# Batch 1's keys and positions loaded a stage ahead, query splits behind the maxima, and layer 1's queries as two 64-column products

## The reference

```python
# layer 1: 16 heads of 64
query = einsum('btd,dnh->bnth', q, w_query) + b_query
weights = softmax(einsum('bnth,bnsh->bnts', query, key) / sqrt(64))
out = einsum('bnth,ndh->btd', weights @ value, w_projection) + b_projection
# layer 2: 16 heads of 8, scores + bias by key position, explicit mask, softmax with a sink of 1
e = exp(scores - max(scores)); attn = e / (1 + sum(e))
# layer 3: 16 heads of 8, triangular and padding mask, plain softmax
```

## Time and profile before

| | us |
|---|---|
| median of 3 runs (lowest, highest) | 1465.39 (1463.68, 1467.89) |
| the profiled execution's own time | 1463.88 |
| its span | 1462.1 |
| busy: PE / DVE / ACT / POOL | 1284.2 / 996.0 / 811.8 / 687.8 |

### The profile page before, as it was taken

The page is one execution under the profiler, slowest core; times in us unless marked ns, Lnnn a source line. Parts: engine busy times, 40 slices in busy tenths (PEclk is TensorE's granted clock), DMA queues, the critical chain, the costliest instruction groups (busy, mean ns, idle before and its releaser), DMA issues. The chain is left out here.

```text
span 1462.1 us, 32229 instructions
## 1 busy us (share of the span) xinstructions
PE 1284.2 (88%) x11864; PEld 764.0 (52%) x11872; DVE 996.0 (68%) x3093; ACT 811.8 (56%) x1191; POOL 687.8 (47%) x630
## 2 busy tenths in 40 slices
PE   6999968836999999999984499999799966999994
PEld 4444444632666666666663145555467752555542
DVE  4988846136667666766557588888365676888866
ACT  2777732333656565656544367777553312777773
POOL 4667613521667667766762445241150027545411
PEclk8999987975999999999996689999999995999997
DMA  4556553534544144323003855440130005534301
GB/s 156 189 221 228 205 200 107 168 101 146 222 152 167 38 159 159 116 86 146 2 1 61 178 125 137 119 122 15 50 59 1 1 8 110 101 78 85 62 7 30
DMA packets 91078, 157.73 MB, mean 108 GB/s; under 512 B 15529, under 2 KB 60740, under 8 KB 87343
## 3 DMA queue, kind: packets, MB, share of 16 engines
q1 hardware_dynamic: 86440, 126.39, 29.8%
q10 hardware_dynamic: 2688, 25.56, 4.5%
q0 software_dynamic: 1808, 3.83, 1.2%
HBM read 99.16 MB, written 50.62 MB: 102 GB/s over the span
## 5 line engine op out<-in xcount | busy, mean ns | idle before, releaser
L2106 DVE CUSTOM_DVE_ANT_0 a_junk<-a_psM,a_madd 128x512 bf16<-128x512 f32 x480 | 312.9, 686 | 64.5 <-issue 57.7
L2049 ACT ACTIVATE a_probs<-a_psE 128x1024 f32<-128x1024 f32 x256 | 262.0, 1024 | 102.2 <-PE a_psE L1907 98.4
L2493 DVE TENSOR_REDUCE a_mx<-a_psM 128x1 f32<-128x512 f32 x236 | 148.2, 669 | 124.4 <-PE a_psM L2317 124.4
L1872 PE MATMUL a_psM<-narrow_k_op,narrow_q_op 57*64 57x512 bf16 (+1 forms) x960 | 194.1, 410 | 13.9 <-DMA narrow_q_op<-a_y_parts 8.7
L2454 ACT ACTIVATE a_probs<-a_psE 128x1024 f32<-128x1024 f32 x128 | 130.8, 1024 | 85.9 <-PE a_psE L2339 82.6
L2287 POOL TENSOR_TENSOR a_half_sum<-a_probs 128x1024 f32<-128x1024 f32 x64 | 150.7, 2355 | 32.7 <-ACT a_probs L2454 32.7
L1919 PE MATMUL a_psO<-a_probs,narrow_values 128*32 128x256 f32 x2048 | 163.7, 393 | 1.2 <-ACT a_probs L2049 1.2
L1898 PE MATMUL a_psE<-narrow_q_op,narrow_k_op 60*64 60x256 bf16 (+1 forms) x2048 | 155.4, 281 | 10.1 <-DMA narrow_q_op<-a_max_parts 10.1
L1907 PE MATMUL a_psE<-a_maddT,res_identb 64*64 64x512 bf16 x512 | 149.2, 386 | 0.0
L1907 PE MATMUL a_psE<-a_maddT_cross,res_identb 64*64 64x512 bf16 x512 | 147.1, 386 | 0.0
L2335 PE MATMUL a_psE<-a_qT,a_kT 64*128 64x256 f32 x1024 | 134.0, 381 | 0.0
(11 more groups left out here) (395 smaller groups left out, 2658.7 us busy)
## 6 DMA issues: line engine op xcount, KB each, us to landing
wide_k<-a_k_stage SPq DMA_DIRECT2D x32, 512.0 KB, 2.6
a_k_part<-wide_k SPq DMA_DIRECT2D x64, 256.0 KB, 2.9
wide_v<-a_v_stage SPq DMA_DIRECT2D x24, 512.0 KB, 4.1
a_kT<-wide_k ACTq DMA_DIRECT2D x6, 2048.0 KB
a_values<-wide_v ACTq DMA_DIRECT2D x6, 2048.0 KB, 8.5
keys<-a_parts SPq DMA_DIRECT2D x96, 64.0 KB
narrow_k_op<-keys SPq DMA_DIRECT2D x30, 192.0 KB
narrow_q_op<-a_queries SPq DMA_DIRECT2D x28, 192.0 KB
```

Source lines behind the costliest of these rows:

```text
L1872: last = pe.matmul(max_bank(s, j, first)[c * n:(c + 1) * n, :], q_op[r][group, s // 2, s % 2 * P + c * n:s % 2 * P + (c + 1) * n], k_op[r] ...
L2049: act.activation(probs[:, head:head + 2, k:k + 2, :], psE[es % 2][:], ACT.Exp).then_inc(exped, 1)
L2106: dve.tensor_tensor_reduce(junk[j][:], max_bank(s, j, first), madd[r][:, t, :], 1.0, -3.0e38, ALU.add, ALU.max, mx[r][:, max_place(h, t):m ...
L2493: dve.tensor_reduce(mx[r][:, at:at + 1], max_bank(2 * p + t, j, first), AX.X, ALU.max).then_inc(max_read, 1)
```

## The change

Three edits. (1) In both narrow layers batch 1's keys (and in layer 2 its positions) are loaded in the stage before, counted by `first_keys`; SP's later list loses them, and batch 1's context and turned mask move behind `maxima(0, 0)`. (2) POOL's `split_queries(v+2)` moves from ahead of `split_max(v, 1)` to the end of the iteration, behind `own_masks(v+2)`. (3) Layer 1's query is two products of 64 columns in two column tiles.

```diff
 # NarrowConstants.sync (int8 block), at its end, before its waits
+        nb.load_keys(sp, self.keys, 1, 1, nb.first_keys)
+        nb.load_positions(sp, 1, 1, nb.first_keys)
 # MaskConstants.gpsimd (layer 2's experts)
-        nb.load_keys(pool, self.keys, 0, 0, nb.first_keys)
+        for u in range(2):
+            nb.load_keys(pool, self.keys, u, u, nb.first_keys)
 # narrow_attention, SP
                 load_mask(1)
-                load_keys(1)
-                load_context(1)
                 load_queries(1)
                 cross_masks(0)
-                load_maskT(1)
 ...
                     maxima(v, 0)
+                    if v == 0:
+                        load_maskT(1)
+                        load_context(1)
 # narrow_attention, POOL
-                    if v + 2 < NCHUNK:
-                        split_queries(v + 2)
                     if cfg.q_bias:
                         bias_batch(v)
                     split_max(v, 1)
                     if v >= 1:
                         normalise(v - 1)
                     if v + 2 < B:
                         own_masks(v + 2)
+                    if v + 2 < NCHUNK:
+                        split_queries(v + 2)
 # narrow_attention, PE
-                            pe.wait_ge(nb.first_keys, 16 * n_keys)
-                        pe.wait_ge(loaded[r], 16 * (n_loads * turn + n_first if r == 0 else n_loads * (turn + 1)))
+                            pe.wait_ge(nb.first_keys, 2 * 16 * n_keys)
+                        pe.wait_ge(loaded[r], 16 * (n_loads * turn + (n_first, 2, n_loads)[r]))
 # layer1_attention, PE
                 def query(v, p):
-                    pe.matmul(psQ, wq[:, p * P:(p + 1) * P], res.xnT[:, bass.ds(v * S, S)], start=True, stop=True).then_inc(q_made, 1)
+                    for j in range(2):
+                        at = p * P + j * WIDE_E
+                        last = pe.matmul(psQ[j * WIDE_E:(j + 1) * WIDE_E, :], wq[:, at:at + WIDE_E], res.xnT[:, bass.ds(v * S, S)],
+                                         start=True, stop=True, tile_position=(0, j * WIDE_E), skip_group_check=True)
+                    last.then_inc(q_made, 1)
```

## The result

| | before | after |
|---|---|---|
| median (lowest, highest), 4 runs each | 1464.54 (1462.42, 1467.89) | 1450.34 (1448.32, 1452.49) |
| span of the profiled execution | 1462.1 | 1448.7 |
| busy: PE / DVE / ACT / POOL | 1284.2 / 996.0 / 811.8 / 687.8 | 1277.3 / 994.8 / 812.1 / 691.7 |

The ratio is 0.9913, 95% interval 0.989 to 0.9936: 12.7 us faster by it, 14.2 by the medians, where 22.6 was forecast. The sign was right and the time inside the range, but it lies 8 us above the forecast and outside the likeliest case's own range, beyond the 1447 that the prediction gave as its own sign of being wrong. Rival B's time, about 1449, is the nearest.

The account below looks back on a forecast made before the run. PE was taken to bound layer 1's attention, and PE's waits on the DMA queue and POOL to cost the narrow layers. Gains of 28.4 less costs of 5.8 gave 22.6 us: 1441.3, stated as 1442, range 1434 to 1453.

Parts of the forecast that it names:

- likeliest case: The forecast itself: 1442 us, with 1437 to 1447 as its own range, chance 0.60.
- 1447: Upper end of the forecast's own range; a time above it, or below 1437, would show the forecast wrong.
- Rival B: Layer 2: queue still holds the maxima, or keys delay the start; 5 to 8 us less gain, about 1449; chance 0.15.
- Layer 1: Two column tiles save 0.20 us per query, 56 times: 11.2 us, plus 2.0 us in batch 0.
- Batch 0's term: Layer 1's first batch: each query 0.25 us shorter in a loop that hides nothing, 2.0 us (0 to 2.4).
- The stalls that go: PE's waits of 10.13 and 2.14 us in layer 2 (11.6 us gain) and 4.76 in layer 3 (3.6 us gain).
- rival D: More than the sum: the clock returns sooner after shorter stalls; 1436 us, chance 0.13.
- part 2: Layer 2's loads moved to the int8 block's end: no delay of first maxima, 0.2 us issue cost, 11.6 us gained.
- The new stalls of part 3: PE waits at batch 2 behind the moved query split: 2.2 us in layer 2, 3.4 in layer 3.
- if the clock falls after it: Condition for the high bound, 8 us, of the batch 2 stalls' cost, counted as 5.6 us in the sum.

Follow-up runs that it names:

- e1: Kernel before with only layer 1's query as two 64-column tiles; 1445.78 against 1456.28 us, ratio 0.9923.
- a0: The changed kernel, unaltered, run again on the second chip; ratio 0.9895 to the kernel before.
- e2: Kernel before with only the narrow layers' edits (early loads, moved query split), layer 1's query still one product; 1454.51 us, ratio 0.9988.
- e3: Changed kernel with the query split of v = 1 back ahead of the second half's maxima, v = 0 still at the end; 0.9838 of the kernel before.
- r3: Same code as e3, run again on the chip of three other runs; ratio 0.9859 to the kernel before.
- e9: Changed kernel with e3's split and batch 1's keys and positions again loaded in the narrow stage, behind batch 1's mask; 0.985 of the kernel before.
- e4: Changed kernel with batch 1's keys and positions for layer 2 loaded on SP behind batch 0's, from the int8 block's start; 0.9925 of the kernel before.
- e7: Changed kernel with e3's split, batch 1's keys loaded by POOL at the int8 block's start, positions early on SP; 0.9896 of the kernel before.
- e12: Changed kernel with e3's split, batch 1's keys loaded by POOL inside the int8 block behind its position cuts, positions early; 0.9858 of the kernel before.
- e11: Changed kernel with e3's split, batch 1's keys loaded by POOL at layer 2's stage start, positions early; 0.9872 of the kernel before.

## Why the prediction was right or wrong

- **Layer 1: the mechanism right, the size partly luck.** It gave 12.35 of 13.2 us. The seven full batches gave 0.194 us a query against 0.20 forecast: 0.15 in the query and 0.04 in the weighing next to it. Batch 0's term, 2.0 us, was mis-sized: its loop gave 0.67, or 0.08 a query where I took 0.25, and another 1.00 us of chance, the clock's earlier return in one step, hid it. The query there takes 1.05 us, not twice 0.43 or 0.45: 0.54 us, the four passes that run into another form, at half the clock, as in the earlier trace rows. I priced batch 0 by the wrong neighbour of that row.
- **The stalls that go: right.** 10.13 to 0, 2.14 to 0.73, 4.76 to 1.10 (forecast 1.1). From first maximum to turn 3 it was 13.54 us where I took 11.6 up to turn 2; 1.38 of it came between turns 2 and 3, where the granted clock is 1.00 after and was 0.74 before in the first 6 us: the clock came back sooner, as rival D had it. Part of the 10.13 was luck of that execution (e1: 6.59).
- **The step that failed: part 2, "Cost 0 (at worst 3 us)"** for the 912 KB sent at the int8 block's end. It cost 4.64 us (3.5 to 4.6 over after, a0, e2, e3, r3), and e9, where it is nothing, shows that moving the loads causes it. Two errors are plain. I took 170 GB/s from a window in which the same loads ran beside masks, context and queries, and at the block's end the engines moved 117 to 121. And I gave slack to the mask alone, while PE's first maximum waits for the first queries' twelve DMAs. How the delay comes about is only half shown: 2.1 to 2.4 us of it stay in e4, e7 and e12, which issue their last load of batch 1 over 7 us ahead of the product, and the order of turned mask and last query that fits them was not tested alone. Rival B named this case with 0.15.
- **The new stalls of part 3: right** to a tenth, 2.22 (2.2) and 3.46 us (3.4). What I kept to the bounds, "if the clock falls after it", happened: 1.49 and 1.46 us. I should have put it in the sum, since I had rows at half clock behind every starved PE.
- **Not in the forecast:** 2.49 us at the end of layer 1, where the same code gives 3.78 or 2.05 us from one execution to the next; 1.18 at turn 4, which comes with the early keys (above; a late DMA of batch 1's maxima would fit, no row names it); and 0.86 up to turn 17, where the kernels spread by 2.4 us (197.14 to 199.54 from turn 16 to 17) for no reason that I found. What decides the first stays open, as does what the transfers share in e11.

The difference closes: 22.6 forecast, less 0.85 (layer 1), 2.49, 4.64, 2.76 (turns 3 to 6), 0.86 (to turn 17) and 1.59 (layer 3), plus 1.94 (first maximum to turn 3), 0.14 (int8 block), 0.06 and 1.16 (before layer 1) gives 12.7, the lead at turn 32 (1415.40 - 1402.67).

## What to carry to other kernels

A load moved into a gap can be paid for by a small transfer with which the next stage starts. Price it at the rate that such loads show, against the first transfer on the path, not the largest; and if the delay doesn't vanish when the load is moved further away, as in e4, look for what else changed its place. An instruction moved on an engine that is off the critical path most of the time should be checked at every iteration it lands in; in layer 3 this one gained 3.7 us in one iteration and lost 5.0 in another. And where one long stall carries the sum, a second execution of the same code says how much of it is always there.

## What the runs showed of the hardware

- While the keys' loads (64 to 192 KB each), the positions and then the first mask were in flight, the engines moved 117 to 121 GB/s at a DMA share of 0.82 to 0.85; about the same share carried more elsewhere (170 GB/s at 0.90, 325 at 0.94 in the changed kernel from 872 to 874 us). Another queue doesn't shield: F 17.81 in e11.
- The time SP needs to issue the same six replicating loads of ones depends on what else is in flight: 9.28 us (e3), 12.20 (e4), 18.81 (e7).
- Behind the stall of 3.5 us at batch 2 of layer 3, a PE at full clock fell to half of it and lost 1.5 us in all four profiles that have it (after, a0, e2, e4); behind the one of 2.2 us in layer 2 in two of the four (13.85 and 15.17 us for the half batch, against 12.33 and 12.34).
- Two 64-column fp32 tiles hold PE 0.48 to 0.54 us at the full clock where one 128-column product holds it 0.63, though the passes are twice as many; at half the clock it is 1.05 against 1.16.
